# One reciprocal and one product for both halves of an attention, in a transformer block on one core

## The reference

```python
x_norm = modulate(_ln(x), shift_a, scale_a)
q, k, v = split(x_norm @ W_qkv + b_qkv)                  # "x": self-attention
attn_out = softmax(q k^T * scale) v                      # 16 heads, 256 x 256 each
x = x + gate_a * (attn_out @ W_proj + b_proj)
q_c = _ln(x) @ W_qc + b_qc                               # "y": cross-attention
k_c, v_c = split(_ln(context) @ W_kvc + b_kvc)
c_attn_out = softmax(q_c k_c^T * scale) v_c
x = x + c_attn_out @ W_cproj + b_cproj
h = gelu(modulate(_ln(x), shift_m, scale_m) @ W_mlp1 + b_mlp1) @ W_mlp2 + b_mlp2
x = x + gate_m * h
```

## Time and profile before

| | us |
|---|---|
| median of 3 runs | 888.11 (887.25 to 888.12) |
| the profiled execution | 888.2 |
| its span | 886.4 |
| PE busy, of the span | 835.9 |
| DVE busy | 622.7 |
| ACT busy | 494.6 |
| POOL busy | 350.8 |

### The profile page before, as it was taken

One profiled execution on the slowest core, in us unless ns is written; L12 is line 12 of the kernel. 1 busy time (PEld: TensorE's weight loads), 2 busy tenths in 40 slices (PEclk: granted clock), 3 DMA queues, 4 the chain that ended last, 5 costly groups with the idle time before them and its releaser, 6 DMA issues.

```text
span 886.4 us, 19236 instructions
## 1 busy us (share of the span) xinstructions
PE 835.9 (94%) x7088; PEld 634.4 (72%) x7088; DVE 622.7 (70%) x1370; ACT 494.6 (56%) x934; POOL 350.8 (40%) x400
## 2 busy tenths in 40 slices
PE   5888999999999999999999999999999999989877
PEld 5656667777787777777787777776786777667656
DVE  4657997787868786877867776877867786763420
ACT  2152657566575756566574756566574755554332
POOL 5444225344262625353451725353352623240322
PEclk9677999999999999999999999999999999999799
DMA  6442232322232232323222332323222232111001
GB/s 227 165 149 74 96 121 73 120 75 88 74 99 89 78 128 73 120 85 99 87 75 80 98 107 73 121 85 102 77 76 85 87 106 85 38 61 36 26 1 37
DMA packets 79784, 79.27 MB, mean 89 GB/s; under 512 B 12681, under 2 KB 74250, under 8 KB 79306
## 3 DMA queue, kind: packets, MB, share of 16 engines
q1 hardware_dynamic: 79402, 77.50, 27.1%
q10 hardware_dynamic: 288, 0.54, 0.2%
HBM read 22.82 MB, written 4.26 MB: 31 GB/s over the span
## 4 chain that ended last, share of the span: by engine, by line
PE 85%; DVE 5%; issue 4%; POOL 2%; ACT 2%; SPq 1%; DMA 1%; POOLq 0%; DVEq 0%; ACTq 0%
PE bank L677 22%; PE scan L766 15%; PE pv L723 13%; PE bank L710 12%; PE bank L701 7%; PE bank L690 5%; PE score L776 5%; PE bank L656 4%; DVE MX_y L1052 1%; SPq L426 1%; DVE MX_x L1052 1%; ACT P L895 1%; DMA gate_m<-d_gate 1%; POOL xn_y L549 1%; DVE PT L966 0%
## 5 line engine op out<-in xcount | busy, mean ns | idle before, releaser
L895 ACT ACTIVATE P<-score 128x512 f32<-128x512 f32 x512 | 286.2, 598 | 212.7 <-PE score L776 209.9
L1052 DVE TENSOR_REDUCE MX_x<-scan 128x2 fp32r<-128x512 f32 x256 | 166.8, 677 | 61.9 <-PE scan L766 61.0
L1052 DVE TENSOR_REDUCE MX_y<-scan 128x2 fp32r<-128x512 f32 x256 | 167.2, 680 | 48.2 <-PE scan L766 48.0
L677 PE MATMUL bank<-xT_y,W 128*128 128x256 f32 x960 | 130.0, 289 | 3.2 <-POOL xT_y L562 1.9
L710 PE MATMUL bank<-w_down,HH 128*128 128x256 f32 x512 | 127.5, 395 | 1.0 <-ACT HH L857 1.0
L677 PEld LDWEIGHTS bank<-xT_y,W 128*128 128x128 f32 x960 | 118.7, 191 | 11.0 <-issue 2.4
L766 PE MATMUL scan<-KS_x,QS_x 63*128 63x256 f32 x512 | 110.9, 328 | 7.6 <-DVE MX_x L1052 4.1
L766 PE MATMUL scan<-KS_y,QS_y 63*128 63x256 f32 x512 | 103.7, 318 | 12.7 <-issue 6.3
L766 PEld LDWEIGHTS scan<-KS_y,QS_y 63*128 63x128 f32 x512 | 71.4, 189 | 60.2 <-issue 35.3
L776 PE MATMUL score<-QS_y,KS_y 64*128 64x256 f32 x512 | 107.4, 317 | 2.8 <-ACT P L895 2.7
L710 PEld LDWEIGHTS bank<-w_down,HH 128*128 128x128 f32 x512 | 94.5, 194 | 19.0 <-ACT HH L857 1.7
(11 more groups left out here) (112 smaller groups left out, 1257.1 us busy)
## 6 DMA issues: line engine op xcount, KB each, us to landing
KS_x<-SK SPq DMA_DIRECT2D x96, 128.0 KB, 2.1
QS_x<-SQ_x SPq DMA_DIRECT2D x96, 128.0 KB, 2.1
KS_y<-SK SPq DMA_DIRECT2D x96, 128.0 KB, 2.6
QS_y<-SQ_y SPq DMA_DIRECT2D x96, 128.0 KB, 2.1
x_in<-in_x SPq DMA_DIRECT2D x16, 256.0 KB, 2.8
c_in<-in_ctx SPq DMA_DIRECT2D x16, 256.0 KB, 3.2
gate_a<-d_gate SPq DMA_DIRECT2D x16, 256.0 KB, 3.5
gate_m<-d_gate SPq DMA_DIRECT2D x16, 256.0 KB, 3.4
```

The costliest lines, as they stand in the source:

```text
L677: last = nc.tensor.matmul(to[:, i * N:(i + 1) * N], w[p][:, c, (blk + i) * 128:(blk + i + 1) * 128], xT[k][:, q, c, :], start=(n == 0), st ...
L895: nc.scalar.activation(P[:, s % 8, :, :].rearrange("p a n -> p (a n)"), score_bank[s % 2][:, :], ACT.Exp, scale=SCALE).then_inc(s_exp, 1)
L1052: nc.vector.tensor_reduce(MX[s1][:, half, col:col + NB], scan_bank[n % NSCAN][:, :].rearrange("p (a n) -> p a n", a=NB), AXIS.X, ALU.max, ...
```

## The change

The four steps stay, but the reciprocal and the product are taken once for both halves. `PT`, `PN` and `rsum` get room for both halves; each half is still transposed into `PT` and back out of `PN` by itself. `pn_x0` and `pn_x1` become `pn_x`, after `pt_x1`; and `po_x0` moves from the end of the section to right behind `pn_x`. The same for y. The matmuls, their order, and the tables of the other engines are unchanged.

```diff
 DVE_PLAN = {
-    "A": [("pt_x1", -1, 0), ("pn_x1", -1, 1), ("max_y1", -2, 2), ("po_x1", -1, 2), ("stats_c", 0, 3), ("out_x", -1,
-          5), ("stats_y", -1, 5), ("norm_y", -1, 7), ("k_x", 1, 8), ("T_y", -1, 8), ("max_x0", 0, 10), ("pt_y0", -2,
-          12), ("q_y", -1, 12), ("pn_y0", -2, 12), ("q_x", 1, 13), ("po_y0", -2, 15), ("pt_y1", -2, 15)],
-    "B": [("pn_y1", -2, 0), ("po_y1", -2, 2), ("down0", -3, 2), ("max_x1", 0, 2), ("T_c", 0, 3), ("out_y", -2, 4),
-          ("stats_m", -2, 5), ("max_y0", -1, 8), ("k_y", 0, 9), ("pt_x0", 0, 11), ("pn_x0", 0, 13), ("down1", -3,
-          13), ("stats_x", 2, 15), ("po_x0", 0, 15)],
+    "A": [("pt_x1", -1, 0), ("pn_x", -1, 1), ("po_x0", -1, 1), ("max_y1", -2, 2), ("po_x1", -1, 2), ("stats_c", 0,
+          3), ("out_x", -1, 5), ("stats_y", -1, 5), ("norm_y", -1, 7), ("k_x", 1, 8), ("T_y", -1, 8), ("max_x0", 0,
+          10), ("pt_y0", -2, 12), ("q_y", -1, 12), ("q_x", 1, 13), ("pt_y1", -2, 15)],
+    "B": [("pn_y", -2, 0), ("po_y0", -2, 0), ("po_y1", -2, 2), ("down0", -3, 2), ("max_x1", 0, 2), ("T_c", 0, 3),
+          ("out_y", -2, 4), ("stats_m", -2, 5), ("max_y0", -1, 8), ("k_y", 0, 9), ("pt_x0", 0, 11), ("down1", -3,
+          13), ("stats_x", 2, 15)],
...
-    "A1": [("pn_x1", -1, 2), ("po_x1", -1, 2), ("stats_c", 0, 6), ("out_x", -1, 6), ("stats_y", -1, 6), ("norm_y",
+    "A1": [("pn_x", -1, 2), ("po_x0", -1, 2), ("po_x1", -1, 2), ("stats_c", 0, 6), ("out_x", -1, 6), ("stats_y", -1,
...
-    "AB-1": [("pt_x1", -1, 0), ("pn_x1", -1, 0), ("po_x1", -1, 3), ("max_y1", -2, 3), ("out_x", -1, 6), ("stats_y",
+    "AB-1": [("pt_x1", -1, 0), ("pn_x", -1, 0), ("po_x0", -1, 0), ("po_x1", -1, 3), ("max_y1", -2, 3), ("out_x", -1,
...
-    "BB+1": [("po_y0", -2, 3), ("pt_y1", -2, 5), ("pn_y1", -2, 5), ("po_y1", -2, 11), ("down0", -3, 14), ("out_y",
+    "BB+1": [("pt_y1", -2, 5), ("pn_y", -2, 5), ("po_y0", -2, 5), ("po_y1", -2, 11), ("down0", -3, 14), ("out_y",
...
-        PT = sb("PT", [128, 2, 8, 32])
-        PN = sb("PN", [128, 8, 2, HD])
+        PT = sb("PT", [128, 4, 8, 32])
+        PN = sb("PN", [128, 8, 4, HD])
...
-        rsum = sb("rsum", [128, 2, 8])
+        rsum = sb("rsum", [128, 4, 8])
...
             def turned(s, half, b):
                 m = half_index(s, b, half)
                 dve.wait_ge(s_pv, 2 * m + 2)
-                wait(dve, s_pn, m)
-                nc.vector.transpose(PT[:, :, :, :].rearrange("p a b c -> p (a b c)"), pv_bank[half % NPV][:, :])\
+                wait(dve, s_pn, m // 2)
+                nc.vector.transpose(PT[:, 2 * half:2 * half + 2, :, :].rearrange("p a b c -> p (a b c)"), pv_bank[half % NPV][:, :])\
                     .then_inc(s_pt, 1)
 
-            def normed(s, half, b):
-                m = half_index(s, b, half)
-                dve.wait_ge(s_pt, m + 1)
+            def normed(s, b):
+                k = half_index(s, b, 0) // 2
+                dve.wait_ge(s_pt, 2 * k + 2)
                 nc.vector.reciprocal(rsum[:, :, :], PT[:, :, :, HD]).then_inc(s_rc, 1)
-                dve.wait_ge(s_rc, m + 1)
-                wait(dve, s_OT, m)
-                nc.vector.tensor_tensor(PN[:, :, :, :].rearrange("p b a d -> p a b d"), PT[:, :, :, 0:HD],
-                                        rsum[:, :, :].unsqueeze(3).to_broadcast([128, 2, 8, HD]),
+                dve.wait_ge(s_rc, k + 1)
+                wait(dve, s_OT, 2 * k)
+                nc.vector.tensor_tensor(PN[:, :, :, :].rearrange("p b q d -> p q b d"), PT[:, :, :, 0:HD],
+                                        rsum[:, :, :].unsqueeze(3).to_broadcast([128, 4, 8, HD]),
                                         ALU.mult).then_inc(s_pn, 1)
...
-                dve.wait_ge(s_pn, m + 1)
-                nc.vector.transpose(OT[:, half, :], PN[:, :, :, :].rearrange("p a b c -> p (a b c)"))\
+                dve.wait_ge(s_pn, m // 2 + 1)
+                nc.vector.transpose(OT[:, half, :].rearrange("p (b c) -> p b c", c=32),
+                                    PN[:, :, 2 * half:2 * half + 2, :].rearrange("p b q d -> p b (q d)"))\
                     .then_inc(s_OT, 1)
```

More of the change, by code:

```diff
@@ L117 @@
     "B0": [("stats_c", 0, 1), ("max_x1", 0, 2), ("k_x", 1, 3), ("q_x", 1, 5), ("T_c", 0, 8), ("pt_x0", 0, 8),
-          ("pn_x0", 0, 9), ("po_x0", 0, 9), ("stats_x", 2, 11), ("k_y", 0, 13), ("pt_x1", 0, 14)],
-    "A1": [("pn_x1", -1, 2), ("po_x1", -1, 2), ("stats_c", 0, 6), ("out_x", -1, 6), ("stats_y", -1, 6), ("norm_y",
[L120 to L123, removed]
@@ L124 @@
-    "AB-1": [("pt_x1", -1, 0), ("pn_x1", -1, 0), ("po_x1", -1, 3), ("max_y1", -2, 3), ("out_x", -1, 6), ("stats_y",
-          -1, 6), ("norm_y", -1, 6), ("max_x0", 0, 9), ("T_y", -1, 9), ("stats_c", 0, 12), ("pt_y0", -2, 13),
-          ("q_y", -1, 13), ("pn_y0", -2, 14), ("po_y0", -2, 15), ("pt_y1", -2, 15), ("T_c", 0, 15), ("pn_y1", -2,
-          15)],
+          ("stats_x", 2, 11), ("k_y", 0, 13), ("pt_x1", 0, 14)],
+    "A1": [("pn_x", -1, 2), ("po_x0", -1, 2), ("po_x1", -1, 2), ("stats_c", 0, 6), ("out_x", -1, 6), ("stats_y", -1,
+          6), ("norm_y", -1, 7), ("k_x", 1, 7), ("T_y", -1, 7), ("max_x0", 0, 9), ("q_y", -1, 11), ("q_x", 1, 13),
+          ("max_x1", 0, 15)],
@@ L128 @@
+    "B1": [("stats_x", 2, 7), ("max_y0", -1, 8), ("T_c", 0, 10), ("pt_x0", 0, 12), ("k_y", 0, 15)],
+    "AB-1": [("pt_x1", -1, 0), ("pn_x", -1, 0), ("po_x0", -1, 0), ("po_x1", -1, 3), ("max_y1", -2, 3), ("out_x", -1,
+          6), ("stats_y", -1, 6), ("norm_y", -1, 6), ("max_x0", 0, 9), ("T_y", -1, 9), ("stats_c", 0, 12), ("pt_y0",
+          -2, 13), ("q_y", -1, 13), ("pt_y1", -2, 15), ("T_c", 0, 15), ("pn_y", -2, 15), ("po_y0", -2, 15)],
     "BB-1": [("max_x1", 0, 1), ("po_y1", -2, 1), ("down0", -3, 6), ("out_y", -2, 8), ("pt_x0", 0, 8), ("max_y0", -1,
@@ L129 @@
           11), ("stats_m", -2, 11), ("k_y", 0, 13)],
[L130 to L134, removed]
+    "AB+0": [("down1", -4, 1), ("pt_x1", -1, 1), ("max_y1", -2, 2), ("pn_x", -1, 7), ("po_x0", -1, 7), ("po_x1", -1,
+          7), ("out_x", -1, 7), ("stats_y", -1, 7), ("norm_y", -1, 7), ("T_y", -1, 9), ("pt_y0", -2, 9), ("q_y", -1,
+          10), ("pt_y1", -2, 11), ("pn_y", -2, 12), ("po_y0", -2, 12), ("po_y1", -2, 15)],
@@ L135 @@
+    "AB+1": [("down1", -4, 8), ("max_y1", -2, 8), ("pt_y0", -2, 15)],
     "AB+2": [("stats_m", -3, 2), ("down1", -4, 2)],
     "BB+0": [("out_y", -2, 2), ("stats_m", -2, 4), ("max_y0", -1, 8), ("down0", -3, 8)],
-    "BB+1": [("po_y0", -2, 3), ("pt_y1", -2, 5), ("pn_y1", -2, 5), ("po_y1", -2, 11), ("down0", -3, 14), ("out_y",
+    "BB+1": [("pt_y1", -2, 5), ("pn_y", -2, 5), ("po_y0", -2, 5), ("po_y1", -2, 11), ("down0", -3, 14), ("out_y",
           -2, 15)],
@@ L1021, in _ @@
                 **{f"{n}_{s}{h}": lambda b, f=f, s=s, h=h: f(s, h, b) for n, f in
-                   (("pt", turned), ("pn", normed), ("po", returned)) for s in "xy" for h in range(2)},
+                   (("pt", turned), ("po", returned)) for s in "xy" for h in range(2)},
+                **{f"pn_{s}": lambda b, s=s: normed(s, b) for s in "xy"},
                 **{f"max_{s}{h}": lambda b, s=s, h=h: maxima(s, h, b) for s in "xy" for h in range(2)},
```

## The result

The changed kernel takes 897.60 us (median; 895.66 to 899.81) beside 888.12 for the kernel before, a ratio of 1.0101 with a 95% interval of 1.0070 to 1.0132. So it is slower by 9.5 us, where 3.6 were predicted: the direction was right and the size was not. The profiled execution took 897.74 us, its span is 895.9 us, and TensorE's mean granted clock was 0.965 (before 0.973).

What follows compares the result with a forecast made beforehand. TensorE was taken to bound the kernel, so VectorE's lateness counts only at uncovered seams: 0.8 + 0.6 + 0.8 + 0.7 + 0.75 - 0.1 = 3.55 us on 888.2, forecast 891.7 us; forecast's own range 889.9 to 894.3, whole range from 887.2.

Steps and rivals of the forecast that it cites:

- Rival 4: Wide pair takes 1.40 us, saving VectorE nothing, and the seams cost 5 us in all: 893 us; chance 0.07.
- 27 hidden seams: Seams where later VectorE work stays covered by other work, so the change costs nothing; steady periods stay at 49.03 us.
- Rival 3: Steady state pays too: GpSimd holds the wide product in each seam, 1.8 us more, 893.5 us; chance 0.05.
- The seam's 0.79: VectorE's lateness behind the last `pt` in a seam: reciprocal +0.11, product +0.26, transpose +0.42, together 0.79 us.
- x of 0: Paid seam at t = 1: VectorE's whole lateness is passed on to `out_x` and the chain behind it, +0.8 us.
- y of 0: Paid seam at t = 2, section B: no `down` covers it, reductions run back to back and `out_y` follows, +0.8 us.
- x of 14: Paid seam at t = 15: product held until GpSimd's subtraction is through, then the extra transpose, +0.7 us.
- y of 15: Paid seam of the last attention: `out_y` waits for the last transpose and everything to the end follows, +0.75 us.
- x of 1: Paid seam at t = 2: +0.8 us for TensorE, about half perhaps absorbed in its wait for `xn_y`; +0.6 us.
- The upper end, slowed throughout: At t = 15, the wide product slowed throughout by GpSimd rather than only held: +1.3 us instead of +0.7.
- Rivals 1 and 2: 1: the burst is absorbed, within 0.2%, 889.6 us, chance 0.16; 2: VectorE's freed time counts, faster, 884 us, chance 0.12.
- the five paid items: Seams in the first and last batches where VectorE is late and its lateness reaches TensorE, +0.6 to +0.8 us each.

Runs made afterwards that it cites:

- e2: Reciprocal and product joined only at the 27 hidden seams, halves separate at the other five: 889.04 us, 1.0003 of the kernel before.
- e1: The changed kernel timed again without an edit: 899.52 us, 1.0113 of the kernel before.
- e9: Reciprocal and product joined only at the seams of x of batches 0 and 1, separate elsewhere: 893.37 us, 1.0032 of the kernel before.
- The four single kernels: Joined at only part of the five paid seams: y of 0; x of 0 and 1; x of 14; y of 15. Ratios to before 1.0044, 1.0032, 1.0013, 1.0028.
- e13: Kernel before plus useless matmuls in TensorE's long waits, 24 instead of 14 at the start: 885.56 us, 0.9964 of the kernel before.
- e12: Kernel before plus useless matmuls in TensorE's long waits, 14 of them at the start: 885.45 us, 0.9948 of the kernel before.

## Why the prediction was wrong in size

- **VectorE's instructions: nearly right.** The reciprocal takes 0.338 us (0.35 predicted), the product 0.70 alone (0.68), 0.762 on average. The transposes back stayed at 0.43. The two groups fell by 9.5 us, not 11.6; busy time fell by 4.2, to 618.5 and not 611, since instructions overlap in that count (the sum over all groups of VectorE fell from 667.0 to 657.4). Rival 4 (a wide pair at 1.40) falls.
- **27 hidden seams: right.** 49.03 us a period, and e2 at 1.0003 [0.9980, 1.0026]. Rival 3 falls.
- **The seam's 0.79 and the waits: right.** Waits for `MX` 12.9 (about 13 predicted), for `OT` 0.9 (1.0). With TensorE kept busy the five seams cost 2.9 us [1.4, 4.0], against 3.55 in the sum. e1's trace gives the items one by one, as the clock at each of these seams is that of the kernel before. From the last `pt` to `out_x` or `out_y` it takes 0.68 us longer for x of 0 (0.8 predicted), 0.89 for y of 0 (0.8), 0.83 for x of 14 (0.7) and 0.70 for y of 15 (0.75). For x of 1 it is 0.89, of which 0.47 is left at the `xn_y` behind it (0.6, half absorbed). Together 3.6 us.
- **x of 14 and GpSimd's hold: right.** The wide product took 1.47 us, 0.19 more than the narrow one, and ended 0.54 us after GpSimd's subtraction of 1.29 us, where the narrow one ended 0.29 after it: 0.25 later (0.26 predicted). The upper end, slowed throughout, did not come. GpSimd's next operation, which the product also overlaps, took 1.71 us (1.45 before). The Trainium skill ("GPSIMD Engine Reference", Specifications, SBUF interfaces) says that GpSimd shares them with VectorE operations of two SBUF inputs. The trace agrees with 1.47 against 0.69 without GpSimd, but the cost of the wider operation in it was small.
- **Rivals 1 and 2: fell.** The loss is far over 0.2%, and e1's seams show all but the 0.4 us of x of 1 passed on; the 2.9 us [1.4, 4.0] alone would not rule out the 1.5 of rival 1. `pt` waits for `pv` longer (33.3 us, 25.4 before), so the freed time came out in front of it.
- **The step that failed: "The whole 0.79 is passed on" and its like in the five paid items.** Each was priced at the lateness of VectorE alone, and everything behind it at the durations of the trace before, which were taken at 2.4 GHz. But these waits stand where TensorE is already thinly used (at t = 2, 1.25 of 2.00 us busy just ahead of it), and with 0.7 to 0.9 us more of idleness the granted clock fell in most of the traces. In the profiled pair `out_y` of t = 2 then cost 1.79 us more, `out_x` of t = 15 1.19, `up` of t = 16 1.41 and the last `down` 1.37, together 5.8. That the last two come from the joining is not shown. Over all executions the clock withheld grew by 6.5 us. The sum of 3.55 put this term at nothing, without a reason; it should have been 6 to 7 us. The trace of before had shown the danger: behind its wait at t = 1 its own `out_x` takes 3.72 us. It stands in its chain of waits:

```profile
69.53 3.72 PE bank L701 x8
```

I took the mean clock of 0.973 as given.

The clock's part can be read from the profiled pair's means too. The clock withheld is (1 - 0.965) x 895.9 = 31.4 us after and (1 - 0.973) x 886.4 = 23.9 before, 7.4 us more (an upper bound, as idle time counts in it). The Trainium skill ("TensorE: Matmul & The Clock Gate", Terms) reckons the penalty so, as throttled time by the share of pulses withheld; the 7 us of the runs agree.

Open: the share of each seam in the clock's part, and what decides whether the clock falls behind a given wait (it did not at t = 2 in e1, and did in e9 with y of 0 not joined). The four single kernels add up, but their intervals are almost as wide as their effects. And the profiled pair differs from its start: the changed kernel's clock over the first 60 us was 0.86 in its profile, 0.80 in the other, and `out_x` of t = 1 began 1.6 us earlier after (67.92, before 69.53). So that pair says little on x of 0 and 1.

## What to carry to other kernels

Where TensorE's use is thin, give a longer wait two prices: the wait itself, and, with a chance of its own, the work behind it at 1.2 GHz. A stretch of the trace before with a clock below 1.00 behind a wait of its own is the warning. Joining small operations saves an engine's time but puts all of it behind the last input; in a seam where that engine is late, the latency counts and the saving does not. If TensorE's waits can't be shortened, a few matmuls without use in them may be worth more than the waits cost: here 0.4 to 0.5% on a tuned kernel.

## What was not expected of the hardware

- In the profiled execution of the changed kernel the longest single wait at the seam of t = 2 was 1.02 us, and the clock fell after it; it then stayed at 1.2 GHz for about 6 us of full use. In e1, the same kernel, it did not fall there.
- Executions of one and the same kernel differ by over 1%, and their mean clock with them: in the group of e13 the kernel before had 885.57 us at 0.977 and 897.75 at 0.962. With 12 executions of a kernel and 23 to 35 of the kernel before, the interval is still 0.2 to 0.3% wide to each side.
- Matmuls that compute nothing of use made the kernel before faster by 0.52% (e12) with 108 more instructions on TensorE.
